# Edge counts gathered in two tables by groups of four tiles, with the keys sent earlier and the rare branch announced

## The chip, the cores and the metric

The kernel runs on one NeuronCore of one Trainium2 chip. The metric is the device time of one execution in microseconds; three runs of the kernel before gave 1151.02, 1152.14 and 1152.32, median 1152.14. One more execution was profiled; its own time and its span stand in the table below. A measurement of this kernel can tell a change from none at about 0.2%.

## What is computed

The input is 625 nodes of 1024 features, 20625 edges (`src`, `dst`, an edge type 0 to 7) and the weights of two layers. What matters here is the first, a relational graph layer, on the layer-normed input `xn`:

```python
out = xn @ root + bias
for r in range(8):
    mask = (edge_type == r)
    sums = segment_sum(xn[src] * mask, dst, 625)
    cnt  = segment_sum(mask, dst, 625)
    out += (sums / max(cnt, 1)) @ weight[r]
```

The kernel turns it round: h[r] = xn @ weight[r] is taken first for all nodes, and then out += (A[r] @ h[r]) / max(cnt, 1), where A[r] is the 625x625 matrix of how many edges of type r go from one node to another. A gate, a quantised linear layer, a graph convolution with the sum of the A[r] and a mixture of eight experts follow. All matrix products keep float32 accuracy by splitting each operand into a high and a low part and multiplying three times (two times with A, whose counts are exact in the high part).

## The kernel before, in words

**Counts.** The eight matrices A[r] lie in one float32 table in HBM, `adj_scratch` (12.5 MB). It is zeroed by 16 DMAs of 767 KB that POOL issues (L1857). Each edge gets a key (dst, type, src) as one number: two operations of DVE (L1280, L1283) after the third chunk of x is normed, one of POOL (L1863) behind the 16 zeroing DMAs, which marks the rows past the last edge. The keys are written to HBM and are read back spread over all partitions, one group of tiles at a time (`key_rows`, L951, issued by ACT, four buffers). The 20625 edges are `TILES` = 162 tiles of 128, in `NG` = 27 groups of `TG` = 6. For each group DVE runs a **key window** (`key_window`, L1238): for each tile an EQ operation (L1248) compares its 128 keys with all 768 of the group and adds up the matches, so that equal keys of a group are merged into one count; two small operations then give the index (`idx`). POOL adds each tile's counts to the table by an indirect, accumulating DMA (L1871). The additions of a group may only start when the last group's have landed, as the same key can occur in both. That wait stands ahead of every group.

**Relation products.** PE runs 9 units (root and eight relations) of two halves. Each half is 8 weight tiles x 5 chunks of rows x 3 products, all through the helper line L482. SP loads four weight tiles at a time into one of two stages (`load`, L371), ACT casts each to its high part (L331), DVE subtracts for the low part (L340), and both parts lie in a ring of 10 tiles. Load g waits until load g-2 is split. Tile t can be split only after PE has used tile t-10. DVE's key windows stand between the splits, behind the tiles with k = 1 and k = 5 of each half, and ACT waits for each of them before it sends for more keys. The first half goes by chunks (L500): chunk c needs x chunk c normed (DVE L1220), transposed (PE L472), cast and subtracted; chunk c+2 is transposed in the middle of chunk c. DVE evicts the root unit's products (L1316), ACT those of the relations (L1007), which then go to `h_scratch`.

**Spread.** Then PE does 24 spreads of 50 products (`spread`, L553): A[r] times a third of h[r]. A[r] comes from the table into one of two buffers, `AT` or `acb` (POOL issues the first two, L1890, SP the others in `adjacency_in`, L410), ACT copies it to `Ar` (`adjacency_copy`, L957, written as L964 in the profile), and POOL adds it to `Atot` (`total`, L1874). `adjacency_copy(0)` stands on ACT ahead of the last five evictions of the relation products. In SP's order, `adjacency_in(2)` stands behind the load of the first third of h[0], and waits for the copy of A[0]; the loads of the second and third third stand behind it.

**Rare branch.** If a count is above 4095, engines run extra work under `e.If` on a flag read from memory (PE L582, DVE L1361, and POOL; a second one for a later step, PE L674). With these inputs the flag is 0 and the long body is skipped.

## Time and profile before

| what | us |
|---|---|
| median of three runs | 1152.14 |
| the profiled execution's own time | 1163.16 |
| its span, first to last instruction | 1161.4 |
| PE busy in the span | 1099.8 |
| root and relation products on PE | 13.3 to 525.7 |
| spreads on PE | 531.3 to 751 |
| gate, quantised layer, convolution, experts | 751 to 1161 |

Times in rows are microseconds from the span's start. A row of a timeline has its start, its length, engine, line, operation, the names it writes and reads, and in brackets how long the engine sat idle before it and what ended that. PE is the matmul queue, PEld its weight loads. A matmul's length includes a pipelined tail, so the distance of two starts is what one costs.

### The profile page before, as it was taken

Reading aid. Unit: us, or ns where it says so; the run is one execution under the profiler, and the core shown is the slowest. Engines: PE = TensorE matmul, PEld = TensorE weight load, DVE = VectorE, ACT = ScalarE, POOL = GpSimd, SP = SyncE. Lnnn points to the kernel's source line nnn. Section 1 sums busy time; section 2 is a strip of 40 time slices with the busy share of each in tenths; the row PEclk is TensorE's granted clock in tenths of the full one; section 3 lists DMA queues with packets and bytes.
Section 4 is the critical chain, followed back from the end, with each engine's and each line's share of the span. In section 5 each row is a group of like instructions: output and inputs, shape, how many; then the busy total and the mean of one; then the engine's idle time right before and its main releaser. Section 6 shows DMA issues by size and latency. Waiting matters only on the chain.

```text
span 1161.4 us, 14333 instructions
## 1 busy us (share of the span) xinstructions
PE 1099.8 (95%) x5505; PEld 920.4 (79%) x5505; DVE 697.3 (60%) x1376; ACT 385.3 (33%) x599; POOL 380.6 (33%) x262
## 2 busy tenths in 40 slices
PE   5999999999999999994999999899979999999896
PEld 4878888888888888884999999887756878888774
DVE  8476666666655652100777676657378748866546
ACT  3222222222222222213223333362333415336652
POOL 6036556456556466651422132000020000310016
PEclk8999999999999999997999999899989999989997
DMA  8965677777666555539665543362242111588757
GB/s 326 416 199 131 157 198 203 204 205 178 160 159 151 120 119 118 112 49 268 186 205 165 176 120 100 103 208 91 73 76 88 30 62 38 218 260 262 246 179 247
DMA packets 84611, 191.77 MB, mean 165 GB/s; under 512 B 29079, under 2 KB 45274, under 8 KB 76088
## 3 DMA queue, kind: packets, MB, share of 16 engines
q1 hardware_dynamic: 36362, 123.40, 33.6%
q0 software_dynamic: 31968, 35.38, 14.4%
q10 hardware_dynamic: 16206, 32.00, 9.4%
q8 instruction: 46, 0.75, 0.3%
q14 instruction: 29, 0.24, 0.1%
HBM read 136.60 MB, written 54.15 MB: 164 GB/s over the span
## 4 chain that ended last, share of the span: by engine, by line
PE 72%; DMA 9%; DVE 8%; POOL 5%; issue 2%; ACT 2%; POOLq 0%; DVEq 0%; SPq 0%
PE ps L482 61%; POOL adj_scratch L1871 5%; DMA stage<-in_w_e 3%; DMA adj_scratch<-cnt,idx 3%; DVE rl L340 2%; PE ps L724 2%; PE ps L761 2%; PE ps L688 2%; DVE EQ L1248 1%; PE ps L472 1%; DMA stage<-h_scratch 1%; ACT rh L331 1%; PE ps L772 1%; DMA stage<-in_w_rel 1%; DMA AT<-adj_scratch 1%
## 5 line engine op out<-in xcount | busy, mean ns | idle before, releaser
L340 DVE TENSOR_TENSOR rl<-stage,rh 128x512 fp32r<-128x512 f32 (+1 forms) x288 | 228.7, 824 | 334.4 <-ACT rh L331 334.4
L331 ACT CAST rh<-stage 128x512 fp32r<-128x512 f32 (+1 forms) x288 | 193.7, 708 | 528.7 <-PE ps L482 289.7
L1871 POOL DMA_INDIRECT adj_scratch<-cnt,idx x162 | 261.5, 1614 | 224.3 <-DMA adj_scratch<-cnt,idx 81.5
L482 PE MATMUL ps<-rh,xTh 128*125 128x512 f32 x800 | 317.1, 396 | 2.0 <-DVE U L1316 1.7
L482 PE MATMUL ps<-rl,xTh 128*125 128x512 f32 x800 | 315.4, 394 | 0.0
L482 PE MATMUL ps<-rh,xTl 128*125 128x512 f32 x800 | 314.9, 394 | 0.0
L482 PE MATMUL ps<-rh,Ar 125*125 125x342 f32 x600 | 194.5, 329 | 20.6 <-DVE rl L340 10.9
L482 PE MATMUL ps<-rl,Ar 125*125 125x342 f32 x600 | 193.5, 327 | 0.0
L482 PEld LDWEIGHTS ps<-rh,xTh 128*125 128x125 f32 x800 | 148.7, 186 | 39.8 <-DVE U L1316 2.1
L482 PEld LDWEIGHTS ps<-rh,xTl 128*125 128x125 f32 x800 | 149.0, 186 | 37.3
L482 PEld LDWEIGHTS ps<-rl,xTh 128*125 128x125 f32 x800 | 149.0, 186 | 36.3
L1248 DVE SCALAR_TENSOR_TENSOR EQ<-KR,kc,later 128x768 bf16<-128x768 f32 x162 | 154.3, 1014 | 0.0
L482 PEld LDWEIGHTS ps<-rh,Ar 125*125 125x125 f32 x600 | 115.5, 192 | 21.7 <-DVE rl L340 11.2
L482 PEld LDWEIGHTS ps<-rl,Ar 125*125 125x125 f32 x600 | 115.6, 193 | 0.0
L1329 DVE SCALAR_TENSOR_TENSOR U<-ps,rc,U 125x342 f32<-125x342 f32 (+1 forms) x120 | 66.2, 569 | 27.3 <-PE ps L482 24.9
L1885 POOL TENSOR_TENSOR Atot<-Atot,Ar 128x3125 f32<-128x3125 f32 x7 | 45.3, 6478 | 102.9 <-ACT Ar L964 102.8
L482 PE MATMUL ps<-rh,uTh 128*125 128x512 f32 x160 | 63.4, 396 | 0.0
L482 PE MATMUL ps<-rl,uTh 128*125 128x512 f32 x160 | 63.1, 394 | 0.0
L482 PE MATMUL ps<-rh,uTl 128*125 128x512 f32 x160 | 63.0, 394 | 0.0
L1908 POOL DMA_DIRECT2D X<-in_fbias x6 | 6.1, 1124 | 161.6 <-ACT U L934 161.6
L1007 ACT COPY He<-ps 125x512 f32<-125x512 f32 x80 | 46.9, 586 | 33.4 <-ACT He L1007 17.4
L472 PE MATMUL ps<-ident,U 125*128 125x125 f32 x160 | 23.0, 294 | 13.6 <-DVE U L1220 13.6
(263 smaller groups left out, 1195.5 us busy)
## 6 DMA issues: line engine op xcount, KB each, us to landing
stage<-in_w_rel SPq DMA_DIRECT2D x32, 1024.0 KB, 6.7
stage<-h_scratch SPq DMA_DIRECT2D x24, 855.0 KB, 6.5
stage<-in_w_e SPq DMA_DIRECT2D x16, 1024.0 KB, 6.1
adj_scratch<-Z POOLq DMA_DIRECT2D x16, 767.0 KB, 22.5
KR<-key_scratch ACTq DMA_DIRECT2D x27, 384.0 KB, 3.7
h_scratch<-He ACTq DMA_DIRECT2D x40, 257.0 KB, 10.1
h_scratch<-He ACTq DMA_DIRECT2D x40, 256.0 KB, 9.0
stage<-in_w_gate SPq DMA_DIRECT2D x8, 1024.0 KB, 6.3
```

The lines of the kernel that those rows point to most:

```text
L331: e.copy(h, s).then_inc(*a_hi.up(*[("hi", t) for t in step(i)]))
L340: e.tensor_tensor(l, s, h.bitcast(F32), ALU.subtract).then_inc(*v_lo.up(*[("lo", t) for t in step(i)]))
L472: ins = e.transpose(ps[:, b, j * P:(j + 1) * P], source[:, c, k * 128:(k + 1) * 128], ident[0:P, 0:P])
L482: ins = e.matmul(ps[0:P, b, 0:width], a, m, start=first and n == 0, stop=last and n == len(parts) - 1)
L688: ins = e.matmul(ps[0:P, b, :], AT[:, k, c * P:(c + 1) * P], m[:, k, HALF[hf]], start=k == 0 and m is gh, stop=k == C - 1 and m is gl)
L724: ins = e.matmul(ps[:, b, 0:vn], a[:, ws], m[:, k, v0:v0 + vn], start=k == 0 and j == 0, stop=k == 7 and j == 2)
L761: ins = e.matmul(ps[0:HC, b, :], a, m, start=k == 0 and q == 0, stop=k == 1 and q == 2)
L1007: e.copy(He[0:P, s % NHE, 2:514], ps[0:P, banks.of["unit", unit, hf, c], :]).then_inc(*a_out.up(("he", unit, c, hf)))
L1248: e.scalar_tensor_tensor(out=EQ[:, j, :], in0=KR[:, g % 4, :], scalar=kc[:, t:t + 1], in1=later[:, j0:j0 + TG * 128], op0=ALU.is_equal, op ...
L1329: e.scalar_tensor_tensor(out=U[:, c, to], in0=ps[0:P, b, cols], scalar=rc[:, r, c:c + 1], in1=U[:, c, to], op0=ALU.mult, op1=ALU.add).then ...
L1871: e.indirect_dma_start(accd, bass.IndirectOffsetOnAxis(ap=idx[:, n:n + 1], axis=0), cnt[:, n:n + 1], None, compute_op=ALU.add).then_inc(*d ...
L1885: e.tensor_tensor(flat, flat, arf, ALU.add).then_inc(*p_row.up(("total", r)))
```

## The change

- Tiles: 162 in groups of 6 become 164 in groups of 4 (41 groups). An EQ compares with 512 keys. Key windows stand behind k = 0, 2, 4 and 6, and the first one stands ahead of the eviction of the last chunk of the first half.
- There are two tables. Groups 0 to 9 go to the first, from then on odd groups go to the second. A group waits only for the last group of its own table. The second table is zeroed by 16 DMAs that SP issues, two behind each of the weight loads 8 to 15; the zeroing of other scratch moves from loads 12 to 21 to loads 16 to 25.
- The adjacency of r is read from the first table and the second is added by an accumulating DMA of POOL (`second_adder`). `adjacency_in(2)` moves behind the load of the last third of h[0].
- The keys are made on DVE ahead of two of the splits of load 1, marked on POOL between the second and third of its zeroing DMAs, sent by SP behind load 3, and the first four groups are read back by SP too.
- Chunk c+1 is transposed in the middle of chunk c, from c = 1 on.
- `gbias` is loaded after the spreads' loads.
- The rare branch of PE and of DVE becomes a compare-and-branch with a hint marked one spread earlier (on DVE ahead of the splits of that spread). The POOL branches and the later ones stay.

```diff
-TILES = 162
-TG = 6
+TILES = 164
+TG = 4
-WINDOWS = (1, 5)
+WINDOWS = (0, 2, 4, 6)
+SOLE = 10
+    accd = [nc.dram_tensor(f"adj_scratch{i}", (ACCN, 1), F32, kind="Internal").ap() for i in range(2)]
+        def if_many(e, name, over, rare):
+            if known:
+                e.br_cmp(e.value_load(many[0:1, 0:1]), 0, f"no_large_counts_{name}", f"large_counts_{name}", "IS_EQ").branch_hint(over)
+                with nc.body(f"large_counts_{name}", valid_engines=[e.engine]):
+                    rare()
+                    e.br(f"no_large_counts_{name}")
+                nc.switch_bb(f"no_large_counts_{name}")
...
+        adder = lambda g: g % 2 if g >= SOLE else 0
+        adjacency = lambda r, i: bass.AP(accd[i].tensor, r * N, [[RI, 128], [P * RI, C], [1, N]])
...
 # sync
-            e.dma_start(BB128[:], gbias.partition_broadcast(128)).then_inc(*d_bb.up(("gbias",)))
             for g in range(2, first("h", 0, 0, 0)):
                 load(g)
-                if 12 <= g < 12 + len(zeros):
+                if g == 3:
+                    on.wait_ge(*at("key rows"))
+                    e.dma_start(keyd.rearrange("(g p) q -> p g q", g=2), kr1[:]).then_inc(*d_key.up(("keys out",)))
+                    on.wait_ge(*at("keys out"))
+                    for kg in range(4):
+                        e.dma_start(KR[:, kg, :], keyflat[kg * TG * 128:(kg + 1) * TG * 128].partition_broadcast(128)).then_inc(
+                            *d_kr_first[kg].up(("kr", kg)))
+                if 8 <= g < 16:
                     on.wait_ge(*at("Z"))
-                    e.dma_start(*zeros[g - 12]).then_inc(*d_slot.up(("slot zero",)))
+                    for a in range(2 * (g - 8), 2 * (g - 7)):
+                        e.dma_start(adj_zeros[1][a], Z[:]).then_inc(*d_zero[1].up(("adj zero", 1)))
+                if 16 <= g < 16 + len(zeros):
+                    on.wait_ge(*at("Z"))
+                    e.dma_start(*zeros[g - 16]).then_inc(*d_slot.up(("slot zero",)))
             for r, q in ORDER:
                 load(first("h", r, q, 0))
-                if q == 0 and r + 2 < R:
+                if q == (2 if r == 0 else 0) and r + 2 < R:
                     adjacency_in(r + 2)
...
 # tensor
-                                 lambda c: turn("n1", c + 2, U, ("n1", "norm", c + 2)) if c + 2 < C else None)
+                                 lambda c: turn("n1", c + 1, U, ("n1", "norm", c + 1)) if 1 <= c < C - 1 else None)
...
+            over_products = e.mark_branch_hint_location()
             spread(R - 1, 1, nothing)
...
 # scalar
-                            if k % 8 in WINDOWS and g < NG:
-                                if g + 4 < NG:
-                                    key_rows(g + 4)
+                            if k % 8 in WINDOWS and g < NG - 1:
+                                if g == 0:
+                                    key_rows(4)
+                                if g + 5 < NG:
+                                    key_rows(g + 5)
                                 g += 1
...
 # vector
+            lows(6)
+            on.wait_ge(*at("edges"))
+            e.scalar_tensor_tensor(out=kr0[:], ...
+            e.scalar_tensor_tensor(out=kr1[:], ...
             lows(8)
...
+                        if unit == 0 and hf == 0 and c == C - 1:
+                            key_window(g)
+                            g += 1
...
 # gpsimd
+            for place in adj_zeros[0][0:2]:
+                e.dma_start(place, Z[:]).then_inc(*d_zero[0].up(("adj zero", 0)))
             on.wait_ge(*at("key sum"))
             e.affine_select(out=kr1[:, 1, :], ...
+            for place in adj_zeros[0][2:]:
+                e.dma_start(place, Z[:]).then_inc(*d_zero[0].up(("adj zero", 0)))
+            for g in range(NG):
+                to = adder(g)
+                on.wait_ge(*at("idx", g))
+                on.wait_ge(*at("cnt", g))
+                on.wait_ge(*at("adj zero", to))
+                if any(adder(b) == to for b in range(g)):
+                    on.wait_ge(*at("added", max(b for b in range(g) if adder(b) == to)))
+                for n in range(g * TG, (g + 1) * TG):
+                    e.indirect_dma_start(accd[to], bass.IndirectOffsetOnAxis(ap=idx[:, n:n + 1], axis=0), cnt[:, n:n + 1], None,
+                                         compute_op=ALU.add).then_inc(*d_acc[to].up(("added", g)))
+            def second_adder(r):
+                on.wait_ge(*at("acb first", r))
+                e.dma_start(acr[r % 2], adjacency(r, 1), accum_op=ALU.add).then_inc(*d_both[r % 2].up(("acb", r)))
...
+            for r in range(2):
+                second_adder(r)
             for r in range(R):
                 total(r)
+                if r + 2 < R:
+                    second_adder(r + 2)
```

## Rows read from the trace of the kernel before

**Rows 1.** The page, part 1: busy time, share of the span, instructions.

```profile
PE 1099.8 (95%) x5505; PEld 920.4 (79%) x5505; DVE 697.3 (60%) x1376; ACT 385.3 (33%) x599; POOL 380.6 (33%) x262
```

**Rows 2.** The chain that ended last, in order of time: start, length, what.

```profile
520.57 7.83 DMA AT<-adj_scratch
...
532.41 15.58 DMA stage<-h_scratch
...
720.41 2.73 PE ps L576 x25
```

**Rows 3.** PE's timeline from the last relation product to the second spread.

```profile
525.45 0.39 PE L482 MATMUL ps<-rh,xTl 128*125 128x512 f32 x1
531.31 0.62 PE L482 MATMUL ps<-rh,Ar 125*125 125x342 f32 x1 [5.47 <-issue]
...
552.60 0.65 PE L482 MATMUL ps<-rh,Ar 125*125 125x342 f32 x1 [10.90 <-DVE rl L340]
```

**Rows 4.** ACT's timeline in the same stretch: the copies of A[0] and A[1].

```profile
528.41 2.80 ACT L964 CAST Ar<-AT 128x3125 fp32r<-128x3125 f32 x1 [18.14 <-DMA AT<-adj_scratch]
...
536.25 2.81 ACT L964 CAST Ar<-acb 128x3125 fp32r<-128x3125 f32 x1 [0.40 <-ACT He L1007]
```

**Rows 5.** POOL's timeline, first two additions of one group, first of the next.

```profile
486.47 1.54 POOL L1871 DMA_INDIRECT adj_scratch<-cnt,idx  x1 [3.55 <-DMA adj_scratch<-cnt,idx]
488.31 1.54 POOL L1871 DMA_INDIRECT adj_scratch<-cnt,idx  x1 [0.30 <-issue]
...
501.75 1.54 POOL L1871 DMA_INDIRECT adj_scratch<-cnt,idx  x1 [4.08 <-DMA adj_scratch<-cnt,idx]
```

**Rows 6.** Line L1871 from 400 to 522 us: from issue to landing.

```profile
DMA to landing us min/median/max: 2.9/3.4/9.6
```

**Rows 7.** The zeroing DMAs of POOL (tile Z, 0 to 66 us): starts and landing.

```profile
L1859 POOL DMA_DIRECT2D adj_scratch<-Z x16: 531/531/793, 17.7 to 26.1; - x16
...
DMA to landing us min/median/max: 9.9/22.5/40.3
```

**Rows 8.** Busy time by stretch in the middle of the spreads: stretch, length, engines, PEclk, DMA share, GB/s.

```profile
600.00:650.00 50.00, 50.00 (x320) 50.00 (x319) 34.60 (x63) 15.71 (x9) 15.41 (x3) 1.00 0.62 182
```

**Rows 9.** DMA issues: KB each, median us from issue to landing.

```profile
X<-in_fbias POOLq DMA_DIRECT2D x4, 512.0 KB, 5.1
```

**Rows 10.** PE's timeline around the transposes of x chunk 2.

```profile
21.92 1.93 PE L472 MATMUL ps<-ident,U 125*128 125x125 f32 x8 [4.31 <-DVE U L1220]
23.50 0.77 PE L482 MATMUL ps<-rh,xTh 128*125 128x512 f32 x1
...
27.88 0.39 PE L482 MATMUL ps<-rl,xTh 128*125 128x512 f32 x1
```

**Rows 11.** The chain from 40 to 90 us: weight load 4.

```profile
54.36 9.07 DMA stage<-in_w_rel
```

**Rows 12.** Two neighbouring EQ operations in DVE's timeline.

```profile
65.92 1.01 DVE L1248 SCALAR_TENSOR_TENSOR EQ<-KR,kc,later 128x768 bf16<-128x768 f32 x1
...
66.86 1.02 DVE L1248 SCALAR_TENSOR_TENSOR EQ<-KR,kc,later 128x768 bf16<-128x768 f32 x1
```

**Rows 13.** PE's timeline, where the first relation unit waits for a bank.

```profile
83.83 0.50 PE L482 MATMUL ps<-rh,xTh 128*125 128x512 f32 x1 [1.67 <-DVE U L1316]
```

**Rows 14.** PE and DVE behind the rare branch of the first step.

```profile
735.26 0.62 PE L482 MATMUL ps<-rh,Ar 125*125 125x342 f32 x1 [4.27 <-issue]
...
735.84 3.10 DVE L340 TENSOR_TENSOR rl<-stage,rh 128x512 fp32r<-128x512 f32 x5 [3.34 <-ACT rh L331]
```

**Rows 15.** ACT's timeline: the cast of gate tile 4.

```profile
734.77 0.62 ACT L331 CAST rh<-stage 128x512 fp32r<-128x512 f32 x1 [2.77 <-DMA stage<-in_w_gate]
```

**Rows 16.** The chain: transposes of the last spread; across PE's later branch, L674 (954.34).

```profile
741.29 0.88 PE ps L472 x8
...
918.85 35.48 PE ps L482 x153
954.34 14.07 PE ps L688 x60
```

More of the change, by code:

```diff
@@ L239, in gnn_ffn_kernel @@
         value_of, counts, known = {}, [], []
+        def if_many(e, name, over, rare):
[5 more added lines that the diff above has]
+                nc.switch_bb(f"no_large_counts_{name}")
+            else:
+                rare()
         def count(name, step=1):
@@ L259, in gnn_ffn_kernel @@
         d_ba, d_bb = count("row_a_in", 16), count("row_b_in", 16)
-        d_zero, d_slot = count("adj_zeroed", 16), count("slots_zeroed", 16)
+        d_zero, d_slot = [count(f"adj_zeroed{i}", 16) for i in range(2)], count("slots_zeroed", 16)
         d_kr = [count(f"key_rows{i}", 16) for i in range(4)]
-        d_acc = count("adj_added", 16)
+        d_kr_first = [count(f"first_key_rows{i}", 16) for i in range(4)]
+        d_acc = [count(f"adj_added{i}", 16) for i in range(2)]
+        d_both = [count(f"adj_both{i}", 16) for i in range(2)]
         d_he = [count(f"h_out{i}", 16) for i in range(NHE)]
@@ L426, in sync @@
             e.dma_start(b1s[:].rearrange("p k n -> p (k n)"), b1).then_inc(*d_sm.up(("small",)))
+            e.dma_start(BB128[:], gbias.partition_broadcast(128)).then_inc(*d_bb.up(("gbias",)))
             for c in range(C):
@@ L581, in tensor @@
             on.wait_ge(*at("flag"))
-            with e.If(e.value_load(many[0:1, 0:1])):
-                many_products(e, Waiter(e), [ev for _, freed in took for ev in freed])
+            if_many(e, "products", over_products, lambda: many_products(e, Waiter(e), [ev for _, freed in took for ev in freed]))
             banks.drop(*[("many", i) for i in range(7)])
@@ L951, in key_rows @@
             def key_rows(g):
-                on.wait_ge(*at("keys out"))
-                if g >= 4:
-                    on.wait_ge(*at("equal", g - 4))
+                on.wait_ge(*at("equal", g - 4))
                 e.dma_start(KR[:, g % 4, :], keyflat[g * TG * 128:(g + 1) * TG * 128].partition_broadcast(128)).then_inc(*d_kr[g % 4].up(("kr", g)))
@@ L981, in scalar @@
                 root("n1", c)
-                if c == 3:
-                    on.wait_ge(*at("key rows"))
-                    e.dma_start(keyd.rearrange("(g p) q -> p g q", g=2), kr1[:]).then_inc(*d_key.up(("keys out",)))
                 turned("n1", c, xTh)
             highs(10)
-            for g in range(4):
-                key_rows(g)
             g, s = 0, 0
@@ L1268, in vector @@
             turned("n1", 1, xTh, xTl)
+            lows(6)
+            on.wait_ge(*at("edges"))
+            e.scalar_tensor_tensor(out=kr0[:], in0=er[0][0:HR], scalar=float(RI), in1=er[1][0:HR], op0=ALU.mult, op1=ALU.add).then_inc(
+                *v_row.up(("key place",)))
+            on.wait_ge(*at("key place"))
+            e.scalar_tensor_tensor(out=kr1[:], in0=er[2][0:HR], scalar=float(N), in1=kr0[:], op0=ALU.mult, op1=ALU.add).then_inc(
+                *v_row.up(("key sum",)))
             lows(8)
@@ L1277, in vector @@
                     normed(c + 1)
-                if c == 2:
-                    on.wait_ge(*at("edges"))
-                    e.scalar_tensor_tensor(out=kr0[:], in0=er[0][0:HR], scalar=float(RI), in1=er[1][0:HR], op0=ALU.mult, op1=ALU.add).then_inc(
-                        *v_row.up(("key place",)))
-                    on.wait_ge(*at("key place"))
-                    e.scalar_tensor_tensor(out=kr1[:], in0=er[2][0:HR], scalar=float(N), in1=kr0[:], op0=ALU.mult, op1=ALU.add).then_inc(
-                        *v_row.up(("key sum",)))
                 if c == 3:
@@ L1360, in vector @@
             on.wait_ge(*at("flag"))
-            with e.If(e.value_load(many[0:1, 0:1])):
-                many_vector(e, Waiter(e))
+            if_many(e, "vector", over_vector, lambda: many_vector(e, Waiter(e)))
             lows(tile["h", R - 1, 2, 0] + RT)
@@ L1856, in pool @@
                 on.wait_ge(*at("x", c))
-            for place in adj_zeros:
-                on.wait_ge(*at("Z"))
-                e.dma_start(place, Z[:]).then_inc(*d_zero.up(("adj zero",)))
+            on.wait_ge(*at("Z"))
+            for place in adj_zeros[0][0:2]:
+                e.dma_start(place, Z[:]).then_inc(*d_zero[0].up(("adj zero", 0)))
             on.wait_ge(*at("key sum"))
@@ L1888, in pool @@
             for r in range(2):
-                on.wait_ge(*at("added", TILES - 1))
-                e.dma_start(acr[r], adjacency(r)).then_inc(*d_adj_first[r].up(("acb", r)))
+                on.wait_ge(*at("added", NG - 2))
+                on.wait_ge(*at("added", NG - 1))
+                e.dma_start(acr[r], adjacency(r, 0)).then_inc(*d_adj_first[r].up(("acb first", r)))
+            for r in range(2):
+                second_adder(r)
             for r in range(R):
                 total(r)
+                if r + 2 < R:
+                    second_adder(r + 2)
             for c in range(C):
@@ L1956, in many_pool @@
                     on.wait_ge(*at("f total", r - 1))
-                e.dma_start(acr[1], adjacency(r)).then_inc(*d_fa.up(("f adj", r)))
+                e.dma_start(acr[1], adjacency(r, 0)).then_inc(*d_fa.up(("f adj first", r)))
+                on.wait_ge(*at("f adj first", r))
+                e.dma_start(acr[1], adjacency(r, 1), accum_op=ALU.add).then_inc(*d_fa.up(("f adj", r)))
                 before = None
```

15 lines of the change are left out of this document (3 added, 12 removed).

## The prediction

> **What bounds the kernel now.** The page's first part comes first: PE is busy for 1099.8 of 1161.4 us [rows 1], so a change can give back only PE's idle stretches and what runs at the lower clock behind them. The chain of waits, read in order of time, then shows where PE was not the last to be ready, and its longest such stretch has an addition table at its head: a load from the table, then a load of h that landed after 15.58 us [rows 2]. PE's own timeline gives the price: the last relation product starts at 525.45, the first spread at 531.31, and the second only at 552.60, after 10.90 us of idleness [rows 3]. ACT's timeline names the cause of the first gap: it sits until 528.41 for A[0], and only then evicts the last five products and copies A[1], from 536.25 on [rows 4]. POOL's timeline shows why A[0] is late: a group of six additions is issued from 486.47 at 1.84 us each, 1.9 in the mean, and the next group starts at 501.75, 15.3 us later, with 4.08 us of it waited for landings [rows 5]; the load of A[0] starts at 520.57 [rows 2]. The second gap is SP's order: the second third of h[0] stands behind `adjacency_in(2)`, which waits for the copy of A[0], and then it shares the DMA engines with two adjacency loads.
>
> **The additions.** Two tables leave the issue at 1.84 to 1.9 us a tile, 7.4 us for a group of four, as a group then waits for the one before last. Landing takes 3.4 us in the median and 9.6 at most [rows 6], so it mostly ends within the other table's 7.4 us. The first additions wait for the zeroing: its last DMA is issued at 26.1 and the slowest takes 40.3 us [rows 7], so they start at about 67. Ten groups on one table cost 7.4 + 5 us each [rows 5], 124 us together; the other 31 cost 229 us. Landed at about 67 + 124 + 229 + 10 = 430, or 440 with some of the landings late. The key windows don't bind: four a half of 27.7 us give one in 6.9 us. The second table's zeroing goes out behind loads 8 to 15, some 85 to 182 us by PE's pace, and lands at about 200, when group 11 wants it. The plain load of A[0] takes 7.83 us [rows 2]. The accumulating load is not in this trace at that size; the nearest row is 512 KB of bias added to X in 5.1 us [rows 9], which scales to 16 us for 1562 KB. A plain load's 7.83 us is the low end. I take 16. All is ready by 480 at the latest, two accumulations one behind the other counted. ACT reaches the first copy at 528.41 - 18.14 = 510.3 [rows 4], 508 with the gain of the start. So this part costs nothing; the cover is some 30 us wide.
>
> **The hand-over to the spreads.** With A[0] copied early, spread 1 starts behind the last product, at 525.7. ACT evicts the last chunk 1 us later, copies A[1] in 2.8 us [rows 4], casts the second third of h[0] (loaded since before 520, as the moved `adjacency_in(2)` no longer stands ahead of it), and DVE subtracts: about 533.5, as spread 1 ends. Before, 22 spreads of 50 products took from 525.7 to 720.4, which is 194.7 us [rows 2, 3]. At the pace of the middle, 320 in 50 us [rows 8], 1100 products take 173 us. That leaves 21.7; I take off 0.4 for the tight first split: **21.3 us**. The cost of the second table here is one accumulating DMA and about 1 us of POOL for each relation, behind `total(r)`, and 1.6 MB more in every 23.6 us, 68 GB/s on top of 182 at a share of 0.62 [rows 8]. It has a relation's time, 23 us, as cover, and only relation 2 is tight: POOL issues its second part when `total(0)` is done, at about 20 us into the spreads, and ACT wants it at 26, with 8 us before PE would feel that. At 8 us it is hidden, at 16 it costs up to 2. I take 0 and keep 2.
>
> **The start.** Chunk 2's transposes move behind half of chunk 1, which removes the idle 4.31 us ahead of 21.92; the slow products go too, ten in 4.4 us from 23.50 to 27.88 [rows 10] where ten at full pace take 2.3. The keys' two operations now sit ahead of two splits and give back 0.9. So the first half ends about 7 us earlier, at 45. That gain isn't handed on whole. Load 4 was issued at 54.36 and took 9.07 [rows 11], and PE then waited until 83.83 for an eviction that stood behind key windows [rows 13]. Load 4 still waits for the splits of tiles 10 and 11, which now stand behind four evictions, key window 0 and the fifth eviction. An EQ on 768 keys costs 0.94 [rows 12]; two thirds of 0.8 and the same rest make 0.68 on 512, so a window of four with its two short operations is 3.2 us. That puts load 4 at 48.5 and its landing at 57.6. From there 20.4 us passed until PE resumed. Now four windows stand in that stretch in place of two: 16 EQ at 0.68 against 12 at 0.94 is 0.4 less, but two more windows bring two casts of 0.62 [rows 15], their hand-overs and two pairs of short operations, 2.1 in all. PE resumes at 57.6 + 22.1 = 79.7, 4.1 earlier, but has stood 4.7 us and runs ten products slow, 2.1 us as above: **2 us** gained. Ends: the keys, now sent through SP's queue behind load 3, come to window 0 later than 43 and the gain turns into a loss of 2; or the chain is lighter than I count and 5 are gained. DVE needs 5 us for two tiles and a window against PE's 6.9, so later halves stay PE's. The 16 zeroing DMAs on SP's queue are 1.5 MB for each weight load's 13.8 us, and the slot zeroing only moves; the extra two tiles are 3.7 us of POOL. These cost nothing while the load's 6 to 9 us of landing have 13.8. `gbias` leaves the crowded start and is wanted only in the gate: nothing.
>
> **The rare branch.** PE stands 4.27 us at the first branch, DVE 3.34 [rows 14]; at PE's later branch, whose skipped body is short, the chain passes from one product to the next within 0.01 us [rows 16]. So reading the flag isn't what costs; going past a long body is. Behind the gap the products run slow. If both hints hide it, PE does two chunks, then waits for DVE. Its five splits took 3.10 us from 735.84 [rows 14]; without the gap four of them are done by then, and the fifth follows the cast of gate tile 4, 734.77 + 0.62 [rows 15]. With the split and an eviction of 0.6 each, PE's transposes start at 736.7 in place of 741.29 [rows 16]. 4.6 us, less up to 1 for the clock: **4 us**; ends 0 and 6.5 (gap and slow products whole). The Trainium skill, Runtime: NRT & Kernel Launch, section on instruction fetch mechanics, says that prefetch is purely sequential and that a taken branch whose target lies outside the window makes the engine fetch it first. The two branches of this trace, 4.27 us and none, agree with its second half. By its first half a hint would bring nothing.
>
> **The sum.** 21.3 + 2 + 4 = 27.3 us off the profiled execution's 1163.2, which makes 1135.9. That execution lies 11.0 above the median of 1152.14, so the median becomes about 1125. Behind 751 all stands relative to PE's end of the spreads and moves with it.
>
> **Rivals.**
> - **The hint does nothing** (0.22): for it, nothing in this trace shows a hinted branch. PE and DVE gaps of 4.3 and 3.3 stay. 1129.
> - **The start or the second table takes back** (0.12): key window 0 waits for keys in the crowded first 60 us, or the accumulating loads land late. The zeroing's 40 us landing [rows 7] speaks for it, the 23 us of cover a relation against it. 4 to 8 us less gain, 1131.
> - **The landing wait stays, and groups of four pay it more often** (0.05): if additions to different tables still go one group after another, 41 groups at 12.4 us from 67 end at 575, against 520.6 before [rows 2], and PE idles: 1152 + 55 + 16 for the second adding + 0 to 10, about 1220 and slower. It decides where the later 31 groups take over about 10 us each, as 67 + 124 + 31 x 10 plus two loads reaches 528. Against it: four additions are issued while one lands in 3.4 [rows 6].
> - **The table isn't what held PE** (0.03): the gap of 10.90 stays as load and split are late anyway. About 1145 to 1150.
>
> The forecast has 0.58. **Range** 1118 to 1135: down by 3 of the start, 2.5 of the branch and 1.5 of rounding; up by the hint's 4, 4 of the start and 2 of the second table. What counts as no change is 0.2%, 1149.8 to 1154.4, as far as a measurement of this kernel can tell. Faster 0.92, same 0.02, slower 0.06.
>
> **What would show it.** No gap of PE between the last relation product and spread 1, and under 1.5 us ahead of spread 2. POOL's groups 7.4 us apart from group 11 on and the last landed by 445. A wait of PE near 75 to 80 us, longer than before's 1.67. Less than 3 us ahead of PE's product behind the branch. Wrong are the steps if the additions end past 508, if ACT waits for an accumulating load among the spreads, or if DVE stands for key rows ahead of window 0.

## The result and the profile after

| kernel | median us (runs) | lowest to highest | ratio to before |
|---|---|---|---|
| before, beside the changed one | 1151.99 (19) | 1143.78 to 1161.73 | |
| changed | 1144.79 (19) | 1138.55 to 1149.23 | 0.9948 (0.9928 to 0.9968) |

The change made the kernel 0.5% faster by the ratio; the medians lie 7.2 us apart. The forecast had the sign right, and its 1125 in a range of 1118 to 1135 was too low, by 20 us. The profiled execution took 1143.56 us, 19.6 less than the one shown of before.

PE's line on the page, beside [rows 1]:

```profile
PE 1096.1 (96%) x5505; PEld 915.6 (80%) x5505; DVE 665.4 (58%) x1408; ACT 390.2 (34%) x599; POOL 392.9 (34%) x272
```

POOL's timeline, the first addition of three groups while the second table is being zeroed, and of three later ones, then the last addition and the first load (beside [rows 5]):

```profile
151.31 1.73 POOL L1898 DMA_INDIRECT adj_scratch<-cnt,idx  x1 [11.54 <-DMA adj_scratch<-cnt,idx]
...
166.86 1.54 POOL L1898 DMA_INDIRECT adj_scratch<-cnt,idx  x1 [8.11 <-DMA adj_scratch<-cnt,idx]
...
182.92 1.63 POOL L1898 DMA_INDIRECT adj_scratch<-cnt,idx  x1 [8.37 <-DMA adj_scratch<-cnt,idx]
...
212.53 1.54 POOL L1898 DMA_INDIRECT adj_scratch<-cnt,idx  x1 [5.29 <-DMA adj_scratch<-cnt,idx]
...
220.09 1.54 POOL L1898 DMA_INDIRECT adj_scratch<-cnt,idx  x1 [0.30 <-issue]
...
227.57 1.54 POOL L1898 DMA_INDIRECT adj_scratch<-cnt,idx  x1 [0.30 <-issue]
...
452.88 1.54 POOL L1898 DMA_INDIRECT adj_scratch<-cnt,idx  x1 [0.30 <-issue]
461.33 0.95 POOL L1922 DMA_DIRECT2D AT<-adj_scratch  x1 [6.92 <-DMA adj_scratch<-cnt,idx]
```

The alternation works as meant. Up to group 10 the groups are up to 19 us apart and wait for a landing; from 212.53 on they are 7.8 us apart in the mean and POOL hardly waits (2.2 us at the most, three times over 1.6). A[0] is loaded at 461.33, where [rows 2] has 520.57.

The hand-over: ACT's copies, POOL's first total, DVE's second split, and PE (beside [rows 3, 4]):

```profile
508.30 2.80 ACT L987 CAST Ar<-AT 128x3125 fp32r<-128x3125 f32 x1
...
526.36 2.80 ACT L987 CAST Ar<-acb 128x3125 fp32r<-128x3125 f32 x1 [0.40 <-ACT He L1027]
529.06 1.62 ACT L344 CAST rh<-stage 125x1710 fp32r<-125x1710 f32 x1
```

```profile
530.52 2.78 POOL L1913 COPY Atot<-Ar 128x3125 f32<-128x3125 f32 x1 [52.02 <-DMA h_scratch<-He]
...
530.71 4.38 DVE L353 TENSOR_TENSOR rl<-stage,rh 125x1710 fp32r<-125x1710 f32 x1 [20.34 <-ACT rh L344]
```

A[0] waits for ACT now, no longer the reverse, and both gaps of [rows 3] are gone but for 3.28 us ahead of the second spread (535.15). Those come from DVE's split, which took 4.38 us where 1.94 is its usual time.

The chain from there to the gate:

```profile
535.15 160.96 PE ps L507 x1010
696.21 6.34 PE ps L507 x40
...
722.80 1.93 PE ps L497 x8
724.73 2.53 PE ps L507 x10
727.26 0.85 PE ps L497 x8
...
740.85 98.76 PE ps L507 x426
```

PE and DVE behind the rare branch (beside [rows 14]):

```profile
713.88 0.39 PE L507 MATMUL ps<-rh,Ar 125*125 125x342 f32 x1 [0.76 <-DVE U L1352]
...
719.16 3.10 DVE L353 TENSOR_TENSOR rl<-stage,rh 128x512 fp32r<-128x512 f32 x5 [4.53 <-issue]
...
722.80 0.47 PE L497 MATMUL ps<-ident,U 125*128 125x125 f32 x1 [5.53 <-DVE U L1352]
```

PE's gap of 4.27 has shrunk to 0.76, but DVE still stands, 4.53, and PE then waits 5.53 us for it.

Where the 19.6 us between the two profiled executions lie, cut at three marks (the end of the last relation product on PE's timeline, 523.58 + 0.23 in the changed kernel, and two of both chains):

| stretch | before | changed | gained |
|---|---|---|---|
| start to the end of the relation products | 525.7 | 523.8 | 1.9 |
| from there through 22 spreads | 194.7 | 178.7 | 16.0 |
| from there to the gate's 426 products | 36.8 | 38.3 | -1.5 |
| from there to the end | 404.2 | 401.0 | 3.2 |

The last row is most likely no work of the change, as this stretch takes anything from 396 to 407 us in the profiles of both kernels and their variants: the chain of before holds four expert weight loads of 7.2 to 11.9 us, the chain after two of 6.7.

### The profile page after: what moved, and what is told of

Read it like the earlier page. It is cut to its first block, busy times and chain, and to the rows that moved or that the text cites. A ratio compares the mean times of both kernels' runs of the same rounds, so it can differ in the third digit from the quotient of the medians.

```text
span 1141.8 us, 14422 instructions
## 1 busy us (share of the span) xinstructions
PE 1096.1 (96%) x5505; PEld 915.6 (80%) x5505; DVE 665.4 (58%) x1408; ACT 390.2 (34%) x599; POOL 392.9 (34%) x272
## 4 chain that ended last, share of the span: by engine, by line
PE 86%; DVE 8%; DMA 3%; ACT 2%; issue 1%; POOLq 0%; ACTq 0%; DVEq 0%; SPq 0%
PE ps L507 71%; PE ps L749 4%; PE ps L786 3%; DVE rl L353 2%; PE ps L713 2%; PE ps L497 1%; DVE EQ L1268 1%; DMA stage<-in_w_e 1%; PE ps L797 1%; PE ps L764 1%; DMA stage<-in_w_rel 1%; ACT rh L344 1%; PE ps L666 1%; PE ps L730 1%; DVE st L1217 1%
## 5 line engine op out<-in xcount | busy, mean ns | idle before, releaser
L353 DVE TENSOR_TENSOR rl<-stage,rh 128x512 fp32r<-128x512 f32 (+1 forms) x288 | 235.0, 834 | 356.7 <-ACT rh L344 339.5
L344 ACT CAST rh<-stage 128x512 fp32r<-128x512 f32 (+1 forms) x288 | 197.3, 707 | 511.2 <-PE ps L507 264.7
L507 PE MATMUL ps<-rh,Ar 125*125 125x342 f32 x600 | 191.5, 324 | 4.0 <-DVE rl L353 3.3
L507 PE MATMUL ps<-rl,Ar 125*125 125x342 f32 x600 | 190.8, 323 | 0.0
L1268 DVE SCALAR_TENSOR_TENSOR EQ<-KR,kc,later 128x512 bf16<-128x512 f32 x164 | 113.5, 747 | 0.0
L507 PEld LDWEIGHTS ps<-rl,Ar 125*125 125x125 f32 x600 | 113.3, 189 | 0.0
L1944 POOL DMA_DIRECT2D X<-in_fbias x6 | 6.0, 1118 | 163.1 <-ACT U L959 163.1
## 6 DMA issues: line engine op xcount, KB each, us to landing
adj_scratch<-Z POOLq DMA_DIRECT2D x16, 767.0 KB, 21.3
```

The costliest lines, as they stand in the source:

```text
L344: e.copy(h, s).then_inc(*a_hi.up(*[("hi", t) for t in step(i)]))
L353: e.tensor_tensor(l, s, h.bitcast(F32), ALU.subtract).then_inc(*v_lo.up(*[("lo", t) for t in step(i)]))
L507: ins = e.matmul(ps[0:P, b, 0:width], a, m, start=first and n == 0, stop=last and n == len(parts) - 1)
L1268: e.scalar_tensor_tensor(out=EQ[:, j, :], in0=KR[:, g % 4, :], scalar=kc[:, t:t + 1], in1=later[:, j0:j0 + TG * 128], op0=ALU.is_equal, op ...
```

## The experiments

### What was late tables worth?

The first theory: the medians of before do not contain the stall that its profiled execution shows. Five kernels, all from before; the first three ran on one chip.

**Before, unchanged.** No edit.

> The kernel before, unchanged, to see one more profiled execution of it. Theory A (the profiled execution of before was not a typical one: its additions ended late, some 10 us later than in a median execution, and that is the stall the forecast counted as recoverable): ratio 1.000 within 0.003; in this profile the additions end some 5 to 10 us before 520 and the second spread starts correspondingly before 552.6, with the execution nearer to 1152. Theory B (the stall is as large in every execution and the second table and the extra zeroing cost elsewhere what they win here): additions end at 518 to 522 again and the second spread starts at 551 to 554.

**Fewer additions.** The last 30 tiles are not added, so the table is ready early; their edges are missing from the adjacency.

```
-            for n in range(TILES):
+            for n in range(132):
```

> The kernel before, where the last 30 of the 162 tiles are not added to the table (that part of the counts is left out), so that the table is ready at about 447 us and not 520. It prices the late table by itself in unprofiled executions. Theory A: the profiled stall was larger than the usual one, 6 to 11 us faster than before, ratio 0.990 to 0.995. Theory B: about 15 us faster as the first profile shows (A[0]'s copy at 510, spread 1 at once, the load behind adjacency_in no longer held up), ratio 0.985 to 0.988.

**The order on SP's queue alone.**

```
-                if q == 0 and r + 2 < R:
+                if q == (2 if r == 0 else 0) and r + 2 < R:
                     adjacency_in(r + 2)
```

> The kernel before with one line of the change alone: adjacency_in(2) stands behind the last third of h[0]. Theory A: the load of the second third no longer waits for the copy of A[0], so the second spread starts 8 to 10 us earlier whatever the table does, ratio 0.991 to 0.994, nearly all that the whole change brought. Theory B: this alone brings about 10 of the 21 us, and the two tables the other 11, ratio 0.991 too, but then e2 is much faster than 0.990. If the ratio is above 0.998, the order is not what held the second spread.

**One group more.** The last six tiles are added twice (those edges count double), a second group behind the last landing. It ran on a second chip.

```
+            for n in range(TILES - TG, TILES):
+                on.wait_ge(*at("added", TILES - 1))
+                e.indirect_dma_start(...)
```

> The kernel before with the last six tiles added a second time behind the others (their counts are doubled), so that the table is ready one group, 14 to 15 us, later in every execution. It turns the lateness of the first profile on by itself. Theory A (lateness costs only beyond what ACT's wait, PE's last products and the load of h cover, and the first profile was beyond it): 10 to 18 us slower than before, ratio 1.009 to 1.016, and the profile shows the two gaps of the first one, about 5 us ahead of spread 1 and about 10 ahead of spread 2. Theory B (a late table costs in proportion from the start, and e2 gained nothing for another reason): 14 us slower too, but then without slack the profile would show PE waiting at spread 1 for all of it.

**Before once more**, on another chip still.

> The kernel before, unchanged. Theory 'its level is set by how late the additions end': where its profile shows the last addition issued by 500 and a gap ahead of the second spread under 3 us, the median lies at 1143 to 1146; where it shows the last addition at 508 or later and a gap of 8 to 11 us, at 1150 or more. Rival 'the level has another cause': the two don't go together.

Measured:

| kernel | A[0] load issued | second spread [gap ahead] | median us | ratio to before (95%) |
|---|---|---|---|---|
| before, as shown | 520.57 | 552.60 [10.90] | 1151.99 | |
| before again | 507.87 | 535.33 [0.83] | 1143.99 | 0.9999 (0.9971 to 1.0027) |
| fewer additions | 428.28 | 538.09 [2.46] | 1143.76 | 0.9993 (0.9969 to 1.0017) |
| order alone | 506.68 | 535.88 [2.58] | 1144.74 | 0.9999 (0.9976 to 1.0021) |
| one group more | 514.34 | 545.48 [10.74] | 1153.1 | 1.0088 (1.0054 to 1.0122) |
| before once more | 494.57 | 532.97 [2.06] | 1144.27 | 1.0009 (0.9987 to 1.0032) |

POOL's, ACT's and PE's timelines of before again:

```profile
497.10 1.54 POOL L1871 DMA_INDIRECT adj_scratch<-cnt,idx  x1 [0.30 <-issue]
507.87 0.96 POOL L1890 DMA_DIRECT2D AT<-adj_scratch  x1 [9.22 <-DMA adj_scratch<-cnt,idx]
...
516.34 2.81 ACT L964 CAST Ar<-AT 128x3125 fp32r<-128x3125 f32 x1 [5.32 <-DMA AT<-adj_scratch]
523.83 0.59 ACT L1007 COPY He<-ps 125x512 f32<-125x512 f32 x1 [4.68 <-PE ps L482]
...
535.33 0.42 PE L482 MATMUL ps<-rh,Ar 125*125 125x342 f32 x1 [0.83 <-DVE rl L340]
```

A[0] lands at 516.3 and is copied by 519.2; ACT then waits 4.68 us for PE. A table 12.7 us earlier than in [rows 2] takes away the whole stall. Fewer additions and the order alone then gained nothing, where both theories of either had expected 6 us or more. With one group more the gap ahead of the second spread is back, 10.74, though none ahead of the first; POOL, ACT, and the chain:

```profile
506.48 1.54 POOL L1876 DMA_INDIRECT adj_scratch<-cnt,idx  x1 [0.30 <-issue]
514.34 0.96 POOL L1895 DMA_DIRECT2D AT<-adj_scratch  x1 [6.32 <-DMA adj_scratch<-cnt,idx]
...
521.87 2.81 ACT L964 CAST Ar<-AT 128x3125 fp32r<-128x3125 f32 x1 [10.60 <-DMA AT<-adj_scratch]
```

```profile
521.87 2.82 ACT Ar L964
...
525.87 15.22 DMA stage<-h_scratch
```

The copy of A[0] ends at 524.7; only then does SP issue `adjacency_in(2)`, and the load of the second third of h[0] behind it starts at 525.87 and lands 15.22 us later. So this gap passes through SP's order, as the prediction said. What the new order is worth by itself with a late table was not run: order alone met an early one.

So the price of lateness is a step with some slack in front of it. A load issued at 494.6 to 507.9 costs nothing (earlier still, at 428, gains nothing), one at 514.3 costs about 10 us in the profile and in the median (10 to 18 had been expected), one at 520.6 about 17 us in the profile (552.60 against 535.33). In six profiled executions (one group more counted without its extra group) the same 162 additions end anywhere from 486.4 to 511.0. POOL's idle time ahead of them is 224.3 us in [rows 5]'s execution, 202.0 to 203.1 in before again, order alone and before out of line (further below), and 194.6 in before once more; by the profile 14 to 18 of the 26 groups behind the first wait for a landing. The kernel before stood close to the edge, and five of the six executions had their own additions on the right side of it.

### Do two tables hide the landings, and is there cover?

**One table.** All 41 groups of four go to the first table; the second stays zero and is still read.

```
-SOLE = 10
+SOLE = 1000
```

> All 41 groups of four are added to the first table (the second stays zero and is still read and added), so every group waits for the landing of the one before it. Theory 'two tables hide the landing': the groups come about 12.4 us apart all the way, so the last lands at 67 + 41 x 12.4 = 575, A[0] some 60 us later than PE wants it: the time is 45 to 60 us over the kernel after. Rival 'the landing was short anyway, groups of four are enough': the groups come under 10 us apart, all is added by 500 and the time is that of the kernel after, within 3 us.

**The second table unread.** Its edges are missing from the adjacency.

```
-            def second_adder(r):
-                on.wait_ge(*at("acb first", r))
-                e.dma_start(acr[r % 2], adjacency(r, 1), accum_op=ALU.add)...
...
-                on.wait_ge(*at("acb", r))
+                on.wait_ge(*at("acb first", r))
```

> The kernel after without the reads of the second table: what is added there is left out of the adjacency, and with it 16 accumulating loads of 1.6 MB. Theory 'the second table costs nothing beyond the traffic': the accumulating loads are hidden behind a relation's products, and the time stays within 2 us of the kernel after (0.998 to 1.002 of it); only the gap ahead of the second spread may shrink. Rival 'the accumulating loads slow the spreads and h loads': the 22 spreads take 3 us less and the time falls by 3 to 6 us.

**Two groups more** in the changed kernel, one for each table (the last four tiles count three times).

```
-            for g in range(NG):
+            for g in [*range(NG), NG, NG + 1]:
```

> The changed kernel, with its last group of four added twice more (one group more for each table; its edges then count three times). Theory 'the changed kernel has cover': A[0]'s load goes out 13 to 20 us later, at 467 to 481, still ahead of 508, and the time is that of the changed kernel within 2 us. Rival 'the cover is used up by the second reads': 4 us or more above it.

One table: 1203.46 us, 1.053 (1.0491 to 1.0569). Its POOL and PE timelines:

```profile
550.15 1.54 POOL L1898 DMA_INDIRECT adj_scratch<-cnt,idx  x1 [0.30 <-issue]
558.05 0.95 POOL L1922 DMA_DIRECT2D AT<-adj_scratch  x1 [6.37 <-DMA adj_scratch<-cnt,idx]
...
579.81 0.62 PE L507 MATMUL ps<-rh,Ar 125*125 125x342 f32 x1 [56.47 <-issue]
```

Groups of four behind one another, the first at 67.6, come (558 - 67.6) / 41 = 12 us apart, as the prediction had it (12.4), and PE stands 56 us. The second table is what makes groups of four possible at all; without it they lose 60 us against the kernel before (1143.4 beside it). Second table unread: 1143.58 us, 1.0004 (0.9983 to 1.0025), and the 1010 products of the spreads took 160.97 us against 160.96. The accumulating loads cost nothing measurable, though the changed kernel itself did not run beside this one. Two groups more: A[0]'s load went out at 481.66, 20 us later than in the profile above, and the time was 1143.28, 0.9991 (0.9971 to 1.0012), beside 1141.77 and 0.9990 of the changed kernel. The changed kernel has the cover that before lacks, where one group cost 10 us. These two groups use it up: A[0] is copied at 509.09, and ACT waited 0.54 us for it.

### The rare branch

**No hints**, twice, on two chips.

```
-            if_many(e, "vector", over_vector, lambda: many_vector(e, Waiter(e)))
+            with e.If(e.value_load(many[0:1, 0:1])):
+                many_vector(e, Waiter(e))
```

(and the same for PE)

> The kernel after with both branches of the first step as they were before, without hints. Theory A (the hint works on PE, but DVE still stands 3 to 5 us at its own branch, and PE waits for DVE): the time is that of after within 0.2%, PE's gap at its branch back at about 4 us, DVE's gap 3 to 5 us. Theory B (the hints gained about 2 us): 2 us slower than after, ratio to before 0.2% above after's 0.9948.

> The changed kernel with plain branches, without both hints. Theory 'PE only exchanges its gap for a longer wait for DVE': PE's gap is 4.1 to 4.5 and it waits under 2 us for DVE afterwards; the time is 0 to 3 us below that of the changed kernel. Rival 'the hints gain': 2 to 4 us above it.

**DVE's hint late**: it stands behind the third chain of spread evictions, just before the branch's own inputs are computed, not ahead of the weight splits.

> The kernel after with DVE's hint marked some 2 us ahead of its branch, behind the evictions, in place of ahead of the splits of a spread. Theory A (DVE holds little code, and what the early hint fetched is overwritten or the fetch isn't made at all): if it was overwritten, the gap falls from 4.5 to 2 to 3 us and 1 to 2 us are gained; if the hint does nothing on DVE, the gap stays at 4 to 5 and the time is after's. Theory B (the early hint worked and the rest is the reading of the flag): the gap is the same or longer.

**The rare bodies out of line**, no hints: PE's and DVE's long bodies stand behind the end of the program and the usual way falls through. On the changed kernel, twice, and on the kernel before.

```
+                e.br_cmp(e.value_load(many[0:1, 0:1]), 0, f"large_counts_{name}", f"no_large_counts_{name}", "IS_NE")
+                nc.switch_bb(f"no_large_counts_{name}")
...
+            tensor(eng, Waiter(eng))
+            far_body(eng, "products")
```

> The kernel after without hints, with the rare bodies of PE and DVE placed behind the end of their programs, so that the common path falls through and takes no long branch. Theory A (what costs is fetching the code behind a long body, and DVE's gap of 4.5 us stayed with the hint): PE's gap falls from 4.1 and DVE's from 4.3 to 4.5 to under 1 us, and with them the slow products behind; 4 to 6 us faster than after, ratio to after about 0.996. Theory B (the gap is the reading of the flag from memory): both gaps stay at 3 to 4.5 us and the time is e4's.

> The kernel before with one edit: the bodies of the rare branch of PE and DVE stand behind the end of the program, so that the usual way falls through. Theory 'the gap is the jump past a long body, and both engines must be rid of it': both gaps fall below 1 us, PE's chain of the gate starts 4 us earlier behind the spreads' end, and the time is 0.9950 to 0.9975 of the kernel before. Rival 'what is gained there is paid elsewhere (PE waits for ACT or for a landing)': within 0.9985 and 1.001.

> The kernel after with both rare bodies behind the end of the program, once more, now beside the same edit of the kernel before. If the tables and the start still bring something by themselves, it is 2 to 4 us below the kernel before with the same edit (the start: PE resumes 2 to 3 us earlier). If it is all the branch, the two agree within 1 us.

**The changed kernel again**, on two more chips, to stand beside them.

> The kernel after, unchanged, in the same job as the next three, as before's level moved between jobs (1152.0 and 1145.7). Theory A (the change wins where the table comes late, and little elsewhere): the ratio to before is 0.995 if before has executions with a late table in this job, and 0.997 to 0.999 if not. Theory B (the change wins the same everywhere): 0.9948 again, within 0.002. In its profile the second spread starts 11 to 13 us behind the last relation product, and DVE stands 4 to 5 us at its branch in spite of the hint.

> The changed kernel, unchanged. Theory: it stays at 1143 to 1145 whatever the kernel before does, as its additions end by 465; the ratio is 0.998 to 1.000 beside a before of 1144 and 0.993 to 0.996 beside one of 1152. Rival 'the change gains everywhere': 0.995 beside a before of 1144 too.

The gaps are from the timelines of PE and DVE, the stretch runs from the end of the 22 spreads to the 426 products. Kernels of one chip letter ran side by side.

| kernel (chip) | PE's gap | PE then waits for DVE | DVE's gap | stretch | median us | ratio to before (95%) |
|---|---|---|---|---|---|---|
| before again (A) | 4.11 | - | 3.35 | 36.6 | 1143.99 | 0.9999 (0.9971 to 1.0027) |
| no hints (A) | 4.14 | - | 4.29 | 36.7 | 1140.78 | 0.9972 (0.9947 to 0.9996) |
| changed (B) | 0.76 | 5.50 | 4.50 | 38.1 | 1142.83 | 0.9986 (0.9964 to 1.0008) |
| hint late (B) | 0.76 | 5.35 | 4.35 | 38.7 | 1144.64 | 1.0004 (0.9980 to 1.0027) |
| changed, out of line (B) | 0.76 | 1.54 | 0.53 | 32.5 | 1140.0 | 0.9975 (0.9949 to 1.0000) |
| before, out of line (C) | 0.76 | 1.53 | 0.53 | 32.4 | 1141.63 | 0.9976 (0.9955 to 0.9997) |
| changed, out of line (C) | 0.76 | 1.53 | 0.53 | 32.5 | 1141.4 | 0.9972 (0.9951 to 0.9993) |
| before once more (D) | 4.15 | - | 3.46 | 35.6 | 1144.27 | 1.0009 (0.9987 to 1.0032) |
| changed (D) | 0.76 | 5.27 | 4.28 | 38.1 | 1141.77 | 0.9990 (0.9968 to 1.0013) |
| no hints (D) | 4.18 | - | 4.48 | 36.9 | 1139.76 | 0.9969 (0.9948 to 0.9990) |

The chain of the kernel without hints (A) beside the one above:

```profile
711.59 3.52 issue
715.11 5.90 PE ps L507 x20
721.00 0.85 PE ps L497 x8
721.86 1.58 PE ps L507 x10
...
737.03 98.76 PE ps L507 x426
```

PE and DVE with both bodies out of line, in the kernel before (C):

```profile
713.82 0.39 PE L500 MATMUL ps<-rh,Ar 125*125 125x342 f32 x1 [0.76 <-DVE U L1347]
718.74 1.07 PE L490 MATMUL ps<-ident,U 125*128 125x125 f32 x8 [1.53 <-DVE U L1347]
...
715.10 3.10 DVE L358 TENSOR_TENSOR rl<-stage,rh 128x512 fp32r<-128x512 f32 x5 [0.53 <-issue]
```

Three readings. First, the hint acts on PE and not on DVE, wherever DVE's stands. Second, removing PE's gap alone gains nothing: the last transposes need DVE's eviction and start as far behind the spreads' end (20.3 us with hints, 722.80 - 702.55; 20.6 without, 721.00 - 700.38). With hints PE idles right ahead of them, and the first eight transposes and ten products run slow, 1.93 + 2.53 us where 0.85 + 1.58 stand without; without hints the slow products lie in the time that DVE needs anyway. Granted clock, from the busy time by stretch of the changed kernel:

```profile
720.00:728.00 8.00, 5.20 (x27) 5.19 (x28) 5.16 (x9) 1.44 (x3) 0.00 (x0) 0.58 0.00 0
728.00:741.00 13.00, 13.00 (x78) 11.42 (x77) 6.75 (x11) 4.46 (x9) 0.00 (x0) 1.00 0.60 200
```

PE had stood 5.53 us ahead of 722.80; the mean of 0.58 over 720 to 728 means that most of it passed at the lower of the two levels, 1.2 GHz, and from 728 on it is 2.4 GHz throughout. Third, with both bodies out of line both gaps go and the stretch shortens by 3 to 4 us against before and by 6 against the changed kernel. The kernels with the bodies out of line and those without hints have the lowest medians measured, 1140.0 to 1141.6 and 1139.8 to 1140.8. Between themselves they were not told apart, as they never ran side by side.

One thing here stays open. Without hints the stretch is 4 us longer than out of line, yet the ratios are the same, 0.997. And the 5.6 us that the stretch gives against the changed kernel on chip B are 2.8 in the medians, where 4 to 6 had been expected. In the profiles the rest of the kernel, from the 426 products to the end, takes 403.9 to 405.5 us in the three out of line, 396.8 and 397.8 in the two without hints, and 400.1 to 402.2 in the changed kernel with hints. These are one execution each; whether part of the gain is paid back there was not found.

That the hints cost about 1.5 us is shown in the profiles (38.1 to 38.7 against 36.7 to 36.9); in medians the one pair side by side (D) differs by 2.0 us, with intervals that overlap, and the changed kernel with hints can't be told from the kernel before on either chip (both intervals hold 1).

## Why the prediction was wrong, step by step

**The step that failed** is the one behind "That execution lies 11.0 above the median of 1152.14, so the median becomes about 1125". The sum of 27.3 us was made against one execution and moved whole to the median. But 21.3 of it was a stall that this execution had and those profiled later did not: four of five executions of before's additions that were profiled (before again, order alone, before once more, before out of line) reach the second spread at 533.0 to 535.9, where the changed kernel reaches it at 534.2 to 536.0. The sign that was there to see: the execution was 11 us above all three runs, and it held a gap of 10.90 us [rows 3] at the end of a chain of landings that vary from 2.9 to 9.6 us [rows 6]. The excess over the median was most likely the stall itself, and should have been taken off it.

The miss of 20 us adds up. 11.0 of it is this step: off the profiled execution itself, 27.3 us make 1135.9. 5.3 is the hand-over, 16.0 in place of 21.3. 5.5 is the branch, a loss of 1.5 in place of a gain of 4. Against these stand the 3.2 us of the last row of the table of stretches, which the prediction did not have. The last 1.2 is that the changed kernel's profiled execution lies 1.2 below its median. Even with the excess taken off, the forecast would have been 9 us too low.

On two further chips the changed kernel was at 0.9986 and 0.9990 of a before that ran at 1143.6 and 1143.9, not told from 1 on either; without hints it was at 0.997 on two. In the first comparison before ran at 1152 and the ratio was 0.9948, while the changed kernel was at 1144.8, 2 to 3 us above its later medians. That the 7 us there are late additions fits the profile shown ahead of the prediction (1163), the highest run of 1161.73, and the one-group-more kernel, which lands on 1153; of before at that level only the execution shown was profiled, and none of the four later comparisons, on four chips, gave the level again (their before ran at 1143.4 to 1145.7), so this remains argued, not shown.

**The additions.** Mostly right. First addition at 65.2 (67 predicted), ten groups on one table in 147 us to 212.5 (124 predicted), 30 later ones 7.8 us apart (7.4). Load of A[0] at 461; by the prediction the last additions had landed at 430 to 440. The missing term is most likely the zeroing of the second table, costed at nothing on SP's queue: it is issued from 89.0 to 187, and between 92 and 212 POOL waits 5.2 to 11.5 us ahead of each group, where 5 were taken. (Two of these waits the profile puts down to DVE, whose key windows are well ahead by then: the fifth is done at 77.5, the fifth group starts at 119.50.) No kernel without this zeroing was run. The cover absorbed it; ACT copied A[0] at 508.3, predicted 508.

**The hand-over**, within the profiled execution: 16.0 us in place of 21.3. Spread 1 did start at once. Of the 5.3 missing, 2.9 are the gap ahead of spread 2, 3.28 where "0.4 for the tight first split" was taken. 2.4 are the pace: "at the pace of the middle, 320 in 50 us, 1100 products take 173 us" was read from one window with none of the slower products behind a wait in it (320 in 50 us would even make 172). The chain's 1010 products in 160.96 us are 0.159 each, and 1100 of them take 175; the granted clock is 0.83 from 530 to 540, where PE stood, and 1.00 from 540 to 600. The accumulating load, put at 16 us, landed in 15.3 in the median and was hidden, as taken.

```profile
DMA to landing us min/median/max: 12.5/15.3/23.8
```

(line L1903 of the changed kernel, all eight such loads.)

**The start.** PE resumed at 79.54 after 4.59 us of waiting (79.7 and 4.7 predicted), load 4 took 9.27 to land at 57.2 (57.6). Of the 4 us gained there, 1.9 were left at the end of the relation products (2 predicted). Over all profiles the last relation product starts at 522.6 to 527.3 in seven kernels made from before, mean 525.4, and at 522.4 to 525.0 in the ten with two tables, mean 523.7, so 2 us are right in the mean, though one pair can show the reverse. The gap ahead of the second spread can take some of them back: with the rare bodies out of line in both, side by side, the changed kernel resumed at 79.48 against 83.48, finished the products 1.2 us earlier, and began the second spread at 534.35 against 534.14. It ended the 22 spreads 0.95 earlier (701.53 against 702.48); the medians agree within 0.3 us.

**The branch.** "If both hints hide it" failed for DVE. The rival "the hint does nothing" (0.22) was nearer and still not it: it does something for PE, and in sum 1.5 us of harm. What the prediction got right is that the gap is the way past a long body: out of line, it goes from 4.1 and 3.4 to 0.76 and 0.53. Its sign, under 3 us ahead of PE's product behind the branch, came true and did not show a gain. The Trainium skill, Runtime: NRT & Kernel Launch, section on instruction fetch mechanics, says that prefetch is sequential and a taken branch to a distant target stalls. The fall-through runs agree. The prediction had drawn from it that a hint would bring nothing; DVE's 4.3 to 4.5 us fit that, PE's 0.76 with a hint does not, and there the measurement decides.

**The rivals.** "The landing wait stays" was priced at about 1220 for a kernel in which one group still waits for the other; built so, it took 1203. In the changed kernel it did not come true, as two tables do overlap. "The table isn't what held PE" (0.03) gave 1145 to 1150, and the result, 1144.8, lies at its edge, but for another reason: in the profiled execution the table did hold PE; in the others nothing did. No rival said that the stall might be missing from most executions, which is the one that was needed.

## What to carry to other kernels

A wait that one profiled execution shows is worth that much only in executions that have it. When the profiled execution is well above the median, look in it for a wait of about that size behind something that varies, and take it off the gain first; one more look at the unchanged kernel settles it. When an engine's gap is to be removed, ask who it waits for next, and remove that engine's gap too; a rare long body can be laid out of line, and that alone, in the kernel before, brought 0.9976 (0.9955 to 0.9997), no less than the whole change on chips on which before ran at 1144 (0.9986 and 0.9990; the intervals overlap).

## What the runs showed of the hardware

**DVE's split waits for POOL's copy.** A split of 125x1710 takes 1.94 us. Where POOL's copy of 128x3125 began first, the split ended 1.8 us behind the copy's end, in all fifteen profiles where that happened. In the order of columns start and length, POOL then DVE, for fewer additions and for before again:

```profile
533.44 2.80 POOL L1882 COPY Atot<-Ar 128x3125 f32<-128x3125 f32 x1 [103.29 <-DMA h_scratch<-He]
...
534.47 3.56 DVE L340 TENSOR_TENSOR rl<-stage,rh 125x1710 fp32r<-125x1710 f32 x1 [20.34 <-ACT rh L331]
```

```profile
536.81 2.80 POOL L1882 COPY Atot<-Ar 128x3125 f32<-128x3125 f32 x1 [27.07 <-DMA h_scratch<-He]
...
533.33 1.94 DVE L340 TENSOR_TENSOR rl<-stage,rh 125x1710 fp32r<-125x1710 f32 x1 [20.34 <-ACT rh L331]
```

In the first, 536.24 + 1.94 = 538.18, and the split ended at 538.03; in the second DVE was first, was done before the copy began, and lost nothing. With a table in time, the gap ahead of the second spread is 0.83 where DVE is first (two profiles) and 2.1 to 3.3 where POOL is, so 1.2 to 2.5 us of chance sit in it. The Trainium skill, SBUF — State Buffer, section "SBUF: two separate sides", says that the port pair shared by the two engines is an exclusive lock held for a whole instruction; these rows agree.

**A branch hint** brought PE's gap of 4.1 to 4.5 us down to 0.76 and left DVE's at 4.3 to 4.5, early or late. Why DVE differs was not found. In the changed kernel DVE's gap without a hint was 4.3 to 4.5 too, in the kernel before 3.3 to 3.5.

**The same additions** ended 25 us apart, 486.4 to 511.0, in profiled executions of one kernel (three unchanged, three with an edit elsewhere).
